# Mixer first, lower tiles' expert outputs beside the sort, gates applied to outputs in the gather loop

## The reference

```
out1 = conv3x3(sign(x + b11), sign(w1) * mean|w1|)   -> batch norm, + x, shift, PReLU, shift
out2 = conv1x1(sign(out1 + b21), sign(w2) * mean|w2|) -> batch norm, + out1, shift, PReLU, shift
```

```
h = tokens @ W_gat                       # 16 numbers a token: 4 heads x 4 experts
e = leaky_relu(a_src[src] + a_dst[dst])  # 524288 edges and a loop for every token
alpha = softmax of e over the edges with one dst;  agg = sum of h[src] * alpha
scores = mean over heads of layernorm(agg + b_gat);  the two best of 4, softmax -> g[token, expert]
out = sum over experts  g[e] * (gelu(x @ W1[e] + b1[e]) @ W2[e] + b2[e])
```

## Time and profile before

| | |
|---|---|
| runs, us | 8342.73, 8344.9, 8347.91 |
| the profiled execution, us | 8360.4 |
| its span, first to last instruction, us | 8358.7 |
| busy share of the span | PE 39%, weight loads 18%, DVE 46%, ACT 24%, POOL 59% |
| sort, from the start to the last DVE instruction | 0 to 1131.6 us |
| places | 1134.5 to 1322 us |
| mixer | 1324 to about 2267 us |
| first and last gather of the loop | 2287.5 and 7741.6 us |
| finishing of the lower tokens | 7766 us to the end |

### The profile page before, as it was taken

How to read it: one execution, slowest core, us unless ns; L and a number is a source line. 1 busy time by engine, 2 the same in 40 slices (tenths; PEclk the granted TensorE clock), 3 DMA queues, 4 the chain that set the end, 5 groups by cost and what they waited for, 6 DMA issues and landing times. The chain is left out here.

```text
span 8358.7 us, 49988 instructions
## 1 busy us (share of the span) xinstructions
PE 3248.3 (39%) x10147; PEld 1491.7 (18%) x10147; DVE 3825.6 (46%) x7442; ACT 2006.1 (24%) x3788; POOL 4891.5 (59%) x4842
## 2 busy tenths in 40 slices
PE   0011005888644443434434344343443444410134
PEld 0011003556411111111111111111111111100001
DVE  9998997888653222222222212222122221221488
ACT  0000004777522222222222222222222222210011
POOL 0000002555477777777777777777777777777552
PEclk9955557888777777767777677777777777765555
DMA  0000002344312121221212212122121221211266
GB/s 20 0 0 0 1 21 64 120 124 124 102 38 45 44 52 38 51 51 38 51 38 51 51 38 51 38 51 51 38 51 38 51 51 38 48 34 17 78 205 219
DMA packets 333987, 464.52 MB, mean 56 GB/s; under 512 B 158255, under 2 KB 233986, under 8 KB 317058
## 3 DMA queue, kind: packets, MB, share of 16 engines
q1 hardware_dynamic: 186282, 406.11, 14.0%
q0 software_dynamic: 147552, 56.95, 7.3%
HBM read 232.79 MB, written 229.93 MB: 55 GB/s over the span
## 5 line engine op out<-in xcount | busy, mean ns | idle before, releaser
L868 POOL DMA_INDIRECT e_got<-rows,e_index x4352 | 4128.3, 949 | 1327.1 <-issue 1327.1
L938 DVE TENSOR_TENSOR e_adv<-e_got,e_near 128x256 f32<-128x256 f32 x68 | 53.7, 789 | 3157.8 <-DMA e_got<-rows,e_index 3157.7
L1397 ACT ACTIVATE ex_hh<-ex_hid_ps,ex_b 128x512 f32<-128x512 f32 x1024 | 697.2, 687 | 1825.4 <-PE ex_hid_ps L1317 1824.6
L1358 PE MATMUL ex_out_ps<-ex_turned,ex_b 36*128 36x512 bf16 x64 | 38.5, 601 | 2634.4 <-DVE ex_o L1410 2634.4
L1416 DVE TENSOR_TENSOR ex_hs<-ex_hh,ex_gate_ps 128x512 f32<-128x512 f32 x512 | 346.1, 686 | 715.5 <-ACT ex_hh L1397 711.6
L1368 PE MATMUL ex_kept_ps<-ex_hh,ex_w 128*128 128x512 f32 x1024 | 548.4, 617 | 273.2 <-ACT ex_kept L1389 273.2
L1363 PE MATMUL ex_out_ps<-ex_hs,ex_w 128*128 128x512 f32 x1024 | 637.0, 707 | 0.6 <-DVE ex_hs L1416 0.6
L710 POOL MEMSET q_word<- 128x128 int16 x1 | 0.2, 205 | 1077.7 <-POOLq L89 1077.7
L1317 PE MATMUL ex_hid_ps<-ex_tn,ex_w 128*128 128x512 f32 x1024 | 577.3, 648 | 0.0
L1317 PE MATMUL ex_hid_ps<-ex_lower,ex_w 128*128 128x512 f32 x1024 | 522.9, 592 | 0.0
L1358 PEld LDWEIGHTS ex_out_ps<-ex_turned,ex_b 36*128 36x128 bf16 x64 | 6.5, 101 | 2686.4 <-DVE ex_o L1410 2686.4
(11 more groups left out here) (381 smaller groups left out, 6352.8 us busy)
## 6 DMA issues: line engine op xcount, KB each, us to landing
e_got<-rows,e_index POOLq DMA_INDIRECT x4352
kept<-ex_kept SPq DMA_DIRECT2D x64, 1024.0 KB
c_kept<-kept SPq DMA_DIRECT2D x64, 1024.0 KB, 5.7
sums<-e_out SPq DMA_DIRECT2D x68, 768.0 KB, 3.7
m_xin<-in_x_dram SPq DMA_DIRECT2D x64, 512.0 KB, 4.4
mid<-m_xm SPq DMA_DIRECT2D x64, 512.0 KB, 2.9
norm<-m_tn SPq DMA_DIRECT2D x64, 512.0 KB, 4.6
ex_tn<-norm SPq DMA_DIRECT2D x64, 256.0 KB, 4.8
```

The source lines that it names most:

```text
L868: pool.indirect_dma_start(got[:, at % 2, c, :], None, rows_d, bass.IndirectOffsetOnAxis(ap=index[:, at % 2, c:c+1], axis=0)).then_inc(S["g ...
L1397: act.activation(self.hh[:, s % 2, :], self.hid_ps[:, s % 2, :], ACT.Gelu, bias=self.b1[:, s % self.GATED // HID, s % HID:s % HID + 1]).th ...
```

## The change

The mixer becomes the first stage, then the sort, the places, the gather loop and the finish.

The sort is now in two blocks. The first builds both key sets, with the flag's reduction; TensorE, ScalarE and SP only load the experts' weights there. The second does all merges. For the lower half it runs with `Outputs`, which makes the lower tiles' expert outputs, all 64 tiles in 65 rounds of 8 gaps. An object `Pace` on each engine puts the sort's units (429 for the 7 levels and the column steps) evenly into the 520 gaps. DVE has no work of `Outputs`, TensorE and ScalarE have it in turns with the transposes and the copies. A crossing has 8 chunks of 512 columns (4 transposes each) in place of 4 of 1024, through a ring of 4 PSUM cells, and is 4 pairs of chunks, one pair to a unit; ScalarE copies 256 columns a chunk.

In the gather loop `Experts` is replaced by `Upper`: only the upper tiles, in turns 4 to 67. The gates of the four quarters are computed in turns 0 to 3 as before, then transposed in fp32 and stored to DRAM; each tile's four gate rows are loaded into all 128 partitions by one broadcast load of 1 MB. ScalarE's Gelu output goes into the second layer without a gate; DVE adds the bias to each expert's output and multiplies by the gate (one instruction with TensorE's result in PSUM), and adds up the four in PSUM.

`hot` in `places` now lies in the memory of `key`. The finish is the same, but for an argument.

```
+class Outputs:
...
+    STEPS, GAPS, AHEAD = EXPERTS * HID, EXPERTS * HID, 3
...
+    def hidden(self, pe, g):
+        r, s = g // self.STEPS, g % self.STEPS
+        if s == 0:
+            pe.wait_ge(self.S["ld%d" % (r % 4)], 16 * (r // 4 + 1))
+        e, f = s // HID, s % HID
+        pe.matmul(self.hid_ps[:, g % 2, :], self.weights.w1[:, e, f*P:(f+1)*P], self.tn[:, r % 4, :], start=True, stop=True).then_inc(self.S["hid"], 1)
+    def tensor(self, pe, r, u):
+        S, last = self.S, self.STEPS * self.TILES
+        if r == 0:
+            self.hidden(pe, 0)
+            self.hidden(pe, 1)
+        for s in range(self.STEPS):
+            g = self.STEPS * r + s
+            if g < last:
+                e, f = s // HID, s % HID
+                pe.wait_ge(S["gel"], g + 1)
+                if f == 0:
+                    need(pe, S["kept"], EXPERTS * r + e - 1)
+                pe.matmul(self.y_ps[:, e % 2, :], self.weights.w2[:, e, f, :], self.hh[:, g % 2, :], start=(f == 0), stop=(f == HID - 1)).then_inc(S["y"], 1)
+                if g + 2 < last:
+                    self.hidden(pe, g + 2)
+            u()
...
+    def scalar(self, act, r, u):
+        S, last = self.S, self.STEPS * self.TILES
+        for s in range(self.STEPS):
+            g = self.STEPS * r + s
+            if g < last:
+                act.wait_ge(S["hid"], g + 1)
+                need(act, S["y"], g - 1)
+                act.activation(self.hh[:, g % 2, :], self.hid_ps[:, g % 2, :], ACT.Gelu,
+                               bias=self.weights.b1[:, s // HID, s % HID:s % HID + 1]).then_inc(S["gel"], 1)
+            if s % HID == 1 and HID <= g <= last + 1:
+                self.keep(act, g // HID - 1)
+            u()
...
+class Pace:
...
+    def __call__(self):
+        self.passed += 1
+        while self.given < self.passed * self.units // self.gaps:
+            next(self.parts, None)
+            self.given += 1
...
+    PAIRS, CELL, RING = 4, 512, 4
+    CHUNK = 2 * PAIRS
...
+                v.wait_ge(iota, 2)
...
+        UNITS = COL_BITS * (COL_BITS + 1) + PART_BITS * (1 + 2 * (PAIRS + 1) + PART_BITS - 1 + 2 * (COL_BITS - 1))
...
             def cross(a, b):
 
                 x = len(crossing_source)
                 crossing_source.append(a)
+                settle()
                 v.sem_inc(to_turn, 1)
-                for c in range(TURN_CHUNKS):
...
+                yield
+                for pair in range(PAIRS):
+                    for c in (2 * pair, 2 * pair + 1):
+                        lo, _ = turned_of(x, c)
+                        olo, ohi = target_of(b, x, c)
+                        hi = copy_of(x, c)
+                        v.wait_ge(copied, CHUNK * x + c + 1)
+                        go(v.tensor_tensor(olo, lo, hi, ALU.min))
+                        go(v.tensor_tensor(ohi, lo, hi, ALU.max))
+                        used[x, c] = count[0]
+                    yield
...
+            def copy(x, c):
+                act.wait_ge(turned, CHUNK * x + c + 1)
+                _, hi = turned_of(x, c)
+                act.activation(copy_of(x, c), hi, ACT.Copy).then_inc(copied, 1)
...
+            def turn(x, c):
+                if c == 0:
+                    pe.wait_ge(to_turn, x + 1)
+                before = used.get((x, c - RING) if c >= RING else (x - 1, CHUNK - RING + c))
+                if before:
+                    pe.wait_ge(done, before)
...
+                for i, g in enumerate(blocks_of(x, c)):
+                    last = pe.transpose(turned_ps[:, c % RING, i*P:(i+1)*P], source[:, g*P:(g+1)*P], ident[:, :])
+                last.then_inc(turned, 1)
...
+class Upper:
...
+    WEIGHINGS, FIRST = 4, 4
...
+    def load(self, sp, at, turn):
+
+        u = (at + 1 - self.FIRST) % 2
+        S, n = self.S, at + 1 - self.FIRST
+        tile = n + 4 * turn
+        sp.dma_start(self.gate[:, u, :, :].rearrange("p e t -> p (e t)"), self.gate_d[tile, :, :].broadcast_to([P, EXPERTS * TOK])).then_inc(S["ld%d" % u], 16)
+        sp.dma_start(self.xm[:, u, :], tile_of(self.mid_d, 1, at, turn, 4, 1 - self.FIRST)).then_inc(S["ld%d" % u], 16)
+        sp.dma_start(self.tn[:, u, :], tile_of(self.norm_d, 1, at, turn, 4, 1 - self.FIRST)).then_inc(S["ld%d" % u], 16)
...
+    def weigh_vector(self, v, k):
+        S, n = self.S, HIS // self.WEIGHINGS
+        need(v, S["gtp"], k)
+        self.gates.vector(v, k, self.agg[:, k*n:(k+1)*n, :], self.ordered[:, :])
+        v.sem_inc(S["gated"], 1)
+        v.wait_ge(S["gtp"], k + 1)
+        need(v, S["gst"], 16 * k)
+        v.tensor_copy(self.rows[:, :], self.acc_ps[:, 0:2*P]).then_inc(S["gtc"], 1)
...
+    def tensor(self, pe, k, at, turn):
...
+            pe.wait_ge(S["gel"], EXPERTS * t + e + 1)
+            need(pe, S["stt"], EXPERTS * t + e)
+            for f in range(HID):
+                last = pe.matmul(self.y_ps[:, :], self.weights.w2[:, e, f, :], self.hh[:, e % 2 * HID + f, :], start=(f == 0), stop=(f == HID - 1))
+            last.then_inc(S["y"], 1)
...
+            v.wait_ge(S["y"], EXPERTS * t + e + 1)
...
+                need(v, S["fin"], t)
+                v.scalar_tensor_tensor(out=self.acc_ps[:, :], in0=self.y_ps[:, :], scalar=self.weights.b2[:, e:e+1], in1=self.gate[:, u, e, :],
+                                       op0=ALU.add, op1=ALU.mult).then_inc(S["stt"], 1)
+                continue
+            need(v, S["add"], (EXPERTS - 1) * t + e - 2)
+            v.scalar_tensor_tensor(out=self.z[:, e % 2, :], in0=self.y_ps[:, :], scalar=self.weights.b2[:, e:e+1], in1=self.gate[:, u, e, :],
+                                   op0=ALU.add, op1=ALU.mult).then_inc(S["stt"], 1)
+            v.wait_ge(S["stt"], EXPERTS * t + e + 1)
+            need(v, S["add"], (EXPERTS - 1) * t + e - 1)
+            v.tensor_tensor(self.acc_ps[:, :], self.acc_ps[:, :], self.z[:, e % 2, :], ALU.add).then_inc(S["add"], 1)
+        v.wait_ge(S["add"], (EXPERTS - 1) * t + EXPERTS - 1)
+        need(v, S["st%d" % u], 16 * ((at - self.FIRST) // 2) + 32 * turn)
+        v.tensor_tensor(self.o[:, u, :], self.acc_ps[:, :], self.xm[:, u, :], ALU.add).then_inc(S["fin"], 1)
 
 def tile_of(d, half, at, turn, unroll, ahead=0):
 
...
-        sorter(nc, edges, keys[0], 0, flag[:, :])
+        mixer(nc, io, dict(xmid=mid, norm=norm, rows=rows.rearrange("(b j p) r -> b p j r", j=H*W//P, p=P), agg=agg[:, :, :], ROW=ROW))
+        weights = Weights(nc, ctx, io)
+        with ExitStack() as c0:
+            sort_keys(nc, edges, keys[0], 0, flag[:, :], Outputs(nc, c0, weights, norm, kept, TOKEN_TILES))
         low = Places(nc, ctx, 0)
         places(nc, keys[0], 0, low)
-        mixer(nc, io, dict(xmid=mid, norm=norm, rows=rows.rearrange("(b j p) r -> b p j r", j=H*W//P, p=P), agg=agg[:, :, :], ROW=ROW))
```

More of the change, by code:

```diff
@@ L447, in sorter, with crossing @@
+        def crossing(x):
+            for pair in range(PAIRS):
+                yield x, pair
+            yield None
+        crossing_source, used = [], {}
         final_low, final_high = [ping], [u_b]
+        if other: other.buffers(ctx)
+        block = ctx.enter_context(nc.Block())
         @block.sync
         def _(sp):
[L451 to L453 removed]
@@ L519, in _ @@
[L519 to L525, removed]
-            for k in range(8):
-                go(v.tensor_scalar(lane[:, k:k+1], lane[:, 0:1], k, 1, ALU.logical_shift_right, ALU.bitwise_and)) if k else None
-            settle()
-            go(v.tensor_scalar(lane[:, 0:1], lane[:, 0:1], 1, None, ALU.bitwise_and)); settle()
@@ L584, in _, with run @@
+            def run(part):
+                for _ in part:
+                    pass
+            final = []
+            sorting_on = sorting()
+            if other:
+                pace = Pace(sorting_on, UNITS, other.ROUNDS * other.GAPS)
+                for r in range(other.ROUNDS):
+                    other.vector(v, r, pace)
+            run(sorting_on)
+            a, b = final
+            settle()
             go(v.tensor_tensor(b[:, :], a[:, :], upper[:, :], ALU.min))
             go(v.tensor_tensor(upper[:, :], a[:, :], upper[:, :], ALU.max)); settle()
-            v.sem_inc(iota_free, 1)
+            v.sem_inc(spent, 1)
@@ new lines, in copying @@
+            def copying():
+                for now in merges():
+                    if now:
+                        x, pair = now
+                        for c in (2 * pair, 2 * pair + 1):
+                            copy(x, c)
+                    yield
+            copying_on = copying()
+            if other:
+                pace = Pace(copying_on, UNITS, other.ROUNDS * other.GAPS)
+                for r in range(other.ROUNDS):
+                    other.scalar(act, r, pace)
+            for _ in copying_on:
+                pass
@@ new lines, in turning @@
+            def turning():
+                for now in merges():
+                    if now:
+                        x, pair = now
+                        for c in (2 * pair, 2 * pair + 1):
+                            turn(x, c)
```

(8 more changed lines are left out.)

714 lines of the change are left out of this document (369 added, 345 removed).

## The result

The changed kernel takes 8479.1 us (median of 4 runs, 8473.61 to 8481.51) against 8345.3 for the kernel before on the same chip (4 runs, 8342.73 to 8347.91): +133.8 us, ratio 1.0159, 95% interval 1.0142 to 1.0177. Forecast were 8474 us, +129. The profiled execution took 8481.17 us, its span is 8479.4.

A forecast was written before the change was run, and what follows sets the result against it. It took POOL's gathers to bound the loop and DVE the sort. Preparation 5.7, crossings 104 and late arrivals 19.5 gave +129 us on the median 8344.9, so 8474 us, range 8398 to 8590.

The forecast's parts named there:

- POOL bounds the loop, the taken work was in its shadow: Gather loop: POOL never waits for data, so removed TensorE and ScalarE work changes 0 us (bounds -26 and +40).
- The gathers beside DVE: Gather loop: two-SBUF-input DVE operations would slow gathers, 77 us by the rule; new ones read one PSUM operand, so 0.
- Mixer first, preparation: Stage order and sort preparation: moving the mixer costs 0; iota wait, flag reduction and block boundary sum to +5.7 us.
- Passes stay at DVE's pace with 8% to spare: Column passes: a unit takes TensorE 2.085 us against 2.265 of DVE, so DVE stays the bound at full clock.
- A crossing takes 15.6 us from its first transpose: Sort's crossings: three 4.4 us intervals plus both ends, 7.4 us more than before, +104 us for 14.
- ScalarE's order is what holds TensorE: Crossings: the next step's Gelu stands behind the pair's copies, which wait for transposes; 4.05 us between pairs with one step.
- TensorE is late at second crossings, 19.5 us in sum: Second crossing of each level: TensorE arrives after DVE, by 3.9 us at k = 1 and 1.7 at k = 7.
- No stall ahead of first crossings: First crossing of each level: TensorE needs 53.3 us and DVE 53.6, so no stall but nothing left.
- Rival (a): Merge phase: TensorE's clock isn't held and it sets the pace, 1151 us against 931; 8571 us in all; chance 0.18.
- Rival (b): Crossings hardly stretch because TensorE finds its Gelu done: 3.7 us each, +69 us, 8414 in all; chance 0.15.
- (c): Gather loop: less load makes gathers shorter, so the kernel gets faster; at 31 ns a gather 8339 us; chance 0.06.
- (d): Whole change does nothing measurable, TensorE being ahead makes up the crossings' stretch: 8352 us; chance 0.05.

The follow-up runs named there:

- experiment 9: Kernel before, old order; operations ahead of a crossing done in two halves of the columns so transposes begin early: 8322.3 us, ratio 0.9967.
- experiment 10: Kernel before with the early transposes, and the sign multiplication also by halves behind the halves of the last column step: 8315.0 us, ratio 0.9957.
- Experiment 1: Changed kernel without the lower tiles' expert steps beside the sort, kept outputs filled with weights: 8349.9 us against 8354.0, ratio 0.9996.
- experiment 2: Changed kernel with ScalarE doing the next step's Gelu ahead of a pair's two copies, not behind them: 8424.0 us, ratio 1.0084 to the kernel before.
- experiment 4: Changed kernel with only 32 of the 64 lower tiles made beside the sort: 8437.5 us, ratio 1.0100 to the kernel before.
- experiment 7: Changed kernel, Gelu ahead of the copies, 203 in place of 189 gaps ahead of the first crossing: 8421.8 us, ratio 1.0087 to the kernel before.

## Why the prediction was right, point by point

- *POOL bounds the loop, the taken work was in its shadow.* Right. The old loop takes 5446.5 and 5445.7 us in experiments 9 and 10, the new one 5445.4 in the changed kernel. Experiment 1's interval leaves room for a gain of 0.14% and a loss of 0.06%, for the loop and all the rest of the change. The floor of a gather was read too sharply: its minimum and median are 943 and 947 ns in the earlier trace rows, 940 and 944 in the changed kernel, and 940 and 944 also with the old loop in experiment 9.
- *The gathers beside DVE.* The term of 0 stands, but the prediction read too much from one row. In the old loop 44 of 4352 gathers take over 1.04 us, 30 of them beside the operations L942, L943 or L947. The 400 that run beside the other DVE operations over two SBUF tiles in that chain (L938, L940, L949 to L951, L958) take 0.95 us at most, so the estimated 77 us have no support there. Beside the new loop's four operations no gather of 529 takes over 0.96.
- *Mixer first, preparation.* Forecast 0 and +5.7. The preparation showed +3.1; DVE waited 3.18 us for the iota, and the block boundary between the two parts cost 0.5 us and not 2.9. The boundary that the prediction took as its price ends a stage, where a store has still to land and the semaphores are cleared; neither is done here. What each of the two is worth, no run shows.
- *Passes stay at DVE's pace with 8% to spare.* Right: the first 78 passes take 353.3 us in both kernels (1048.22 to 1401.51 after), at a clock of 1.00 from 1100 to 1200 us, and TensorE was done 21 us ahead of DVE.
- *A crossing takes 15.6 us from its first transpose.* 16.0 in the one shown (1992.31 to 2008.32), 15.7 on average at levels 2 to 7. The interval was 3.91 for 4.05; the share of double steps was 12 of 42 for 21%. The errors cancel: 3.91 + 0.29 x 1.72 = 4.41 against 4.4. That is luck.
- *ScalarE's order is what holds TensorE.* Shown by experiment 2, which takes 1.31 us out of each interval.
- *TensorE is late at second crossings, 19.5 us in sum.* It is late, by 0.9 to 3.1 us at levels 2 to 7 (DVE's first wait of 2.2 to 4.4 us against 1.2 at first crossings), 12 us in sum there where the prediction's formula gives 15.7. Level 1 cost 3.5 more than written, and the two offset each other: luck again.
- *No stall ahead of first crossings.* Right but for level 5, where TensorE was 0.6 us late. And I priced the first of all at full clock. TensorE had stood idle for 21 us there and began at 1.2 GHz, enough for the 3.5 us of level 1 (its first interval took 6.6 us for 3.91):

```profile
1403.97 1.97 PE L876 MATMUL s_turned<-s_ident,s_ping 128*128 128x128 f32 x8 [20.95 <-DVEq L748]
...
1406.99 2.08 PE L506 MATMUL o_y_ps<-o_hh,w_w 128*128 128x512 f32 x2 [1.05 <-ACT o_hh L524]
```

- *Rival (a), the clock isn't held.* Not so: 1.00 from 1413 us on, with a stop of 1.05 us at every pair:

```profile
1413.00:2088.00 675.00, 609.06 (x1704) 287.24 (x1704) 517.06 (x414) 345.21 (x588) 0.00 (x0) 1.00 0.22 79
```

The Trainium skill's rule on short gaps between matmul groups (TensorE: Matmul & The Clock Gate, "A second HAM failure mode: psum-queue depth-cycling") didn't show in this kernel. The clock did matter where TensorE stood still for longer ahead of a crossing: 20 us and more in experiment 4, and only 2.0 to 4.0 us in experiments 2 and 7.
- *Rival (b), TensorE finds its Gelu done.* Not in this order of ScalarE; experiment 2 is that rival made true, at +70 us for its +69, with an interval of 2.60 + 0.29 x 1.72 = 3.1 us for its 3.17.
- *Rivals (c) and (d).* (d), no change, is refuted by the result: the merges take 1054.7 us, not 931. (c), a gain in the loop, is refuted by experiment 1: without the steps the time is that of before, and a gather still comes every 1.253 us.

## What to carry to other kernels

Work that fits beside a bound engine by its sum can still cost where that engine hands over to the shared ones: look at each hand-over, and ask what stands in the fixed order between request and answer. Here it paid to have the filler ahead of a hand-over or behind it and not between its pieces, and to do the filler's own Gelu ahead of the copies and not behind them. Even so the best order still cost 37 us. Work that is hidden already, as here under the gathers, had nothing to gain from a move.

## What I had not expected of the hardware

- Half the filler gave back only 50 of the 134 us: TensorE went idle, its clock was 0.80 on average from 1600 to 1800 us, and the crossings took 13.9 us where 11.2 were expected. Tripled matmuls of no use then gave back 19 us more.
- At full clock eight fp32 transposes have a row of 1.04 us, but the next matmul starts 0.88 us after their first when it is ready; 32 in a row take 4.50. A price for a chain has to be taken from start to start.
- The old gather loop had 947 and 949 ns a gather in two executions, 10 us in all, the new one took 5443 to 5451 us over its nine profiles, and the mixer 943 to 952 over all twelve.
